# A third H buffer, stores queued ahead of zero fills, sums from tile 195, and a segment product from split F32R operands

## The chip, the core and the metric

The kernel runs on one core of a Trainium2 chip. A core has TensorE (PE), VectorE (DVE), ScalarE (ACT), GpSimd (POOL), SyncE (SP, which here only issues DMAs) and 16 DMA engines. The metric is the device time of one execution in microseconds (us).

## What is computed

Two graph layers over 50,000 nodes of 256 features and 25,000 edges sorted by target, each with a residual and a layer norm:

```python
neighbor_sum = segment_sum(x[col], row)            # edges -> their target nodes
mean_neighbor = neighbor_sum / max(deg, 1)
h_mean = (x + mean_neighbor) * 0.5 @ W_mean + b_mean
h_concat = concat([x @ W_ego + b_ego, mean_neighbor @ W_nb + b_nb])
gate = sigmoid(gate_weight * node_vec + gate_bias)
x = layernorm(x + (1 - gate) * h_mean + gate * h_concat)
# then an attention layer over the same edges (4 heads), and layernorm(x + it)
```

All of it is float32. What is changed here belongs to the first layer: the products of x (node tiles) and of the mean neighbour (edge tiles).

## The kernel before

**Stages.** A setup block loads weights and constants and starts sorting the edges. The node stage works on 391 node tiles of 128 rows. The edge stage behind it does the second layer and the outputs; the change leaves its code alone.

**Node tiles.** Tiles come in halves of HALF = 5, 78 halves and one last tile. SP loads a half of x into X (XB = 3 buffers, L468). TensorE transposes two tiles at a time (`turn`, L925), ACT copies them to xT (`copy_x`), TensorE multiplies each with w_node, 384 columns, into one of three PSUM banks (`product`, L937), which ACT has filled with the biases before (`seed`, L571). DVE adds x and the gated part into H (`first`, L665, and `add`, L677) and takes statistics (`stat`). H has two buffers of a half each; SP stores a finished half into hc_tab (`store`, L477). `first` waits, at the first tile of a half, until the store of the same buffer has landed.

**Zeros.** The other 384 columns of each row of hc_tab must be zero where a node has no edge. SP fills them from zero_row: rows 0 to 60 of each partition in the setup, then one `clear` (L482) for each half, 28 rows three times and then 7 rows each, by the table CLEARS. SP's order for half h is: load(h+3), clear(h+1), store(h). load(h+3) waits until half h has been read from X, store(h) until half h is complete. All three go on one hardware queue.

**Edge tiles.** 196 tiles of 128 edges, in 98 pairs. GpSimd gathers the edges' data (L518), then x[col] into xg (`fetch`, L522). DVE forms running sums acc (`run_sum`, L852). TensorE transposes a pair's sums into bank 4 (`turn_sum`, L963), ACT copies them to accT (`copy_sum`, L595), TensorE multiplies each tile with w_nb, 384 columns (`product_sum`, L973), ACT scales the result into cn (`main_part`, L602), and GpSimd scatters cn into hc_tab (`put`, L531). GpSimd's order is written out: put(t-13), then fetch(t). The first put waits until all zeros have landed.

**The order between the two.** The work on pairs is put by hand into the steps of the node tiles. A pair p begins at step SUMS + p * SPAN // 98, with SUMS = 188 and SPAN = 186: its running sums come in that step on DVE, its turn and copy two steps later (LATE = 2), its products two pairs after that (LAG_P = 2). From step FIX = 378 on a few instructions mend rows that cross partitions. DVE, ACT and TensorE each work through their steps in order, so an instruction that waits holds up all behind it on its engine.

Of the kernel before, what the change touches and what calls it, by code (L numbers as in the profile page):

```python
# [9 lines left out]
P, D = 128, 256  # L10
# [3 lines left out]
HALF = 5  # L14
# [79 lines left out]
def build(nc, x, src, dst, edge_weight, node_vec, W_mean, b_mean, W_ego, b_ego, W_nb, b_nb, gate_weight,  # L94
# [10 lines left out]
    with ExitStack() as ctx:  # L105
        def sb(n, s, d=F32):
            return ctx.enter_context(nc.sbuf_tensor(n, s, d))
# [35 lines left out]
        gwb = sb("gwb", [P, 2])  # L143
        w_node = sb("w_node", [P, 2, 384])
        w_nb = sb("w_nb", [P, 2, 384])
        w1f = sb("w1f", [P, 2, HEADS * HID])
        w1h = sb("w1h", [P, 2, HEADS * HID], F16)
        w1l = sb("w1l", [P, 2, HEADS * HID], F16)
# [38 lines left out]
        opened = sem("opened")  # L187

        c_zeroed = sem("c_zeroed")
        CLEARS = (0, 60, 88, 116) + tuple(range(144, NT, 7)) + (NT,)  # L190
        c_main = hc_tab[0:P * NT, 0:U].rearrange("(p t) d -> p t d", p=P)
        rows_merged, rec_out, ident_ready = sem("rows_merged"), sem("rec_out"), sem("ident_ready")
        XB = 3
        rows = ExitStack()
        X = [rows.enter_context(nc.sbuf_tensor(f"X{s}", [P, HALF, D], F32)) for s in range(XB)]
        x_in = [sem(f"x_in{s}") for s in range(XB)]
# [15 lines left out]
        with nc.Block() as block:  # L212
# [90 lines left out]
            def _(dve):  # L303
# [53 lines left out]
                st.wait()  # L357
                st.done(v.tensor_copy(w_nb[:, :, 0:256], w_node[:, :, 0:256]))
                st.wait()
                dve_at[0] = st.base + st.n  # L360

            @block.tensor
# [11 lines left out]


        TEN = 2 * HALF
        H = [tmp(f"H{s}", [P, HALF, HU]) for s in range(2)]
        XR = 4
        xT = [tmp(f"xT{b}", [P, 2, D]) for b in range(XR)]
        stats = tmp("stats", [P, TEN, 6])  # L380
        mv = tmp("mv", [P, TEN, 2])
        var_s = tmp("var_s", [P, TEN])
        sd_s = tmp("sd_s", [P, TEN])
        h_out = [sem(f"h_out{s}") for s in range(2)]
# [38 lines left out]
        accT = [tmp(f"accT{b}", [P, 2, D]) for b in range(AR)]  # L423
        carry = tmp("carry", [P, D])
        head_c = tmp("head_c", [P, U])
        carry_c = tmp("carry_c", [P, U])
# [8 lines left out]
        LASTR = (ET - 1) % AC  # L435
        PUT_LAG = 13

        SORT, PHASES, DECODE, SUMS, SPAN, FIX = 0, 7, 16, 188, 186, 378
        PRODS = (5, 6, 7)
        LEAD_X, LAG_P, LATE = 4, 2, 2  # L440

# [23 lines left out]
        with nc.Block() as block:  # L465
            @block.sync
            def _(sp):
                def load(h):  # L468
                    if h >= XB:
                        sp.wait_ge(a_done, (h - XB + 1) * HALF)  # L470
                    if h < 2 * ITER:
                        sp.dma_start(X[h % XB][:, :, :], x_main[:, h * HALF:(h + 1) * HALF, :])\
                            .then_inc(x_in[h % XB], 16)
                    else:
                        sp.dma_start(X[h % XB][:, 0, :], x[N - P:N]).then_inc(x_in[h % XB], 16)

                def store(j, s):  # L477
                    sp.wait_ge(h_done, j * TEN + (s + 1) * HALF)
                    sp.dma_start(h_main[:, bass.ds(j * TEN + s * HALF, HALF), :], H[s][:, :, :])\
                        .then_inc(h_out[s], 16)  # L480

                def clear(c):  # L482
                    lo, hi = CLEARS[c], CLEARS[c + 1]
                    sp.dma_start(c_main[:, lo:hi, :],
                                 zero_row[:, :].unsqueeze(1).to_broadcast([P, hi - lo, U])).then_inc(c_zeroed, 16)

                def half(j, s):
                    if 2 * j + s + XB <= 2 * ITER:
                        load(2 * j + s + XB)
                    if 2 * j + s < len(CLEARS) - 2:  # L490
                        clear(2 * j + s + 1)
                    store(j, s)

                for j in range(ITER):
                    for s in range(2):
                        half(j, s)
                for s in range(2):
                    sp.wait_ge(h_out[s], 16 * ITER)
                sp.wait_ge(h_done, NT + 1)
                sp.dma_start(hc_tab[N - P:N, U:RU], H[0][:, 0, :]).then_inc(h_out[0], 16)  # L500
                sp.wait_ge(h_out[0], 16 * ITER + 16)

            @block.gpsimd
            def _(pool):
# [55 lines left out]
            def _(act):  # L560
# [55 lines left out]
                def side(j, i):  # L616
                    now = j * TEN + i
                    if sorting(now):
                        m, part_ = phase_of(now)
                        if part_:  # L620
                            keep_upper(m)
                        else:
                            reverse_rows(m)
                            keep_back(m)
                    for p in tiles_of(now, LATE):
                        sums(p)
                    if now == FIX + 1:
                        act.wait_ge(carry_ready, 1)
                        a.activation(carry[:, :], bank[4][:, 0:D], ACT.Copy).then_inc(carry_out, 1)
                    if now == FIX + 3:  # L630
                        act.wait_ge(turned, PAIRS + 1)
                        a.activation(accT[0][:, 0, :], bank[5][:, 0:D], ACT.Copy).then_inc(turned_out, 1)

                def round_(j):
                    for i in range(TEN):
# [25 lines left out]
            def _(dve):  # L661
# [1 line left out]
                st = Steps(dve, dve1, dve_at[0])  # L663

                def first(t, i):  # L665
                    s, k = i // HALF, i % HALF
                    dve.wait_ge(p_ready, t + 1)
                    if t >= TEN and k == 0:
                        dve.wait_ge(h_out[s], (t - i) // TEN * 16)
                    if k == 0:  # L670
                        many = HALF if not isinstance(t, int) or t < NT else 1
                        v.tensor_copy(H[s][:, 0:many, D:D + 3], gates[:, bass.ds(t, many), :])
                    v.scalar_tensor_tensor(out=H[s][:, k, 0:D], in0=bank[NODE[t % 3]][:, 0:D],  # L673
                                           scalar=gates[:, bass.ds(t, 1), 1], in1=X[t // HALF % XB][:, k, :], op0=ALU.mult,
                                           op1=ALU.add).then_inc(a_done, 1)

                def add(t, i):  # L677
                    s, k = i // HALF, i % HALF
                    dve.wait_ge(a_done, t + 1)
                    v.scalar_tensor_tensor(out=H[s][:, k, 0:D], in0=bank[NODE[t % 3]][:, D:2 * D],  # L680
                                           scalar=gates[:, bass.ds(t, 1), 2], in1=H[s][:, k, 0:D], op0=ALU.mult,
                                           op1=ALU.add).then_inc(h_done, 1)

                def stat(t, i):
                    s, k = i // HALF, i % HALF
# [144 lines left out]
                def fix_degree():  # L830
# [31 lines left out]
                def side(j, i):  # L862
# [10 lines left out]
                        tables()  # L873
                    if now == DECODE + 2:
                        shares()
                    for p in tiles_of(now):
                        if p < PAIRS:
                            run_sum(2 * p, 2 * p % RS, 2 * p // RS)
                            run_sum(2 * p + 1, (2 * p + 1) % RS, 2 * p // RS)
# [3 lines left out]
                        {0: fix_rows, 2: fix_degree, 5: fix_sum}[now - FIX]()  # L883

                hround = [0]
                for s in range(2):
                    v.memset(H[s][:, :, D + 3:HU], 0.0)

                def round_(j):
                    hround[0] = j  # L890
# [31 lines left out]
            def _(pe):  # L922
# [40 lines left out]
                def turn_sum(p):  # L963
                    pe.wait_ge(acc_ready, 2 * p + 2)
                    if p:
                        pe.wait_ge(turned_out, p)
                    for t in (2 * p, 2 * p + 1):
                        for c in range(2):
                            o = t % 2 * D + c * P
                            ins = t_.transpose(bank[4][:, o:o + P], acc[t % AC][:, c * P:(c + 1) * P], ident[:, :])  # L970
                    ins.then_inc(turned, 1)

                def product_sum(t):  # L973
                    pe.wait_ge(turned_out, t // 2 + 1)
                    if t >= 3:
                        pe.wait_ge(cn_ready, t - 2)
                    for c in range(2):
# [24 lines left out]
                def product_carry():  # L1002
                    pe.wait_ge(turned_out, PAIRS + 1)
                    for c in range(2):
                        ins = t_.matmul(bank[6][:, 0:384], accT[0][:, 0, c * P:(c + 1) * P], w_nb[:, c, :],
                                        start=c == 0, stop=c == 1)
                    ins.then_inc(prod_ready, 1)

# [921 lines left out]
```

## Time and profile before

| | us |
|---|---|
| median of 3 runs | 2945.29 |
| the three runs | 2940.87, 2945.29, 7257.4 |
| profiled execution | 2944.66 |
| its span, first to last instruction | 2942.9 |
| mean granted TensorE clock in it | 0.973 of full |

The node stage takes about 27 to 1030 us of the span, the edge stage the rest. A time in the trace is counted from the start of the span. DMA share is the mean busy share of the 16 DMA engines as the packets' times add up, and can come out a little above 1.

### The profile page before, as it was taken

What the parts mean: (1) busy time and instruction counts of PE and PEld (TensorE: products, weight loads), DVE (VectorE), ACT (ScalarE), POOL (GpSimd) and SP (SyncE); (2) the same over time, 40 slices, a digit from 0 to 9 for tenths busy, and PEclk for the clock granted to TensorE, in tenths of its full rate; (3) what the DMA queues carried; (4) which work ended last, traced back from release to release, by engine and by line L of the source; (5) the groups of instructions that cost most, each with busy time, mean ns of one, the idle gap of its engine ahead of it and who ended that gap; (6) DMA issues with size and microseconds to landing.
All of it is one profiled execution on the core that took longest, in us unless ns stands there. A gap on an engine that the chain in (4) does not pass through costs nothing. (4 is left out here: it accounts for less than half of the span.)

```text
span 2942.9 us, 52181 instructions
## 1 busy us (share of the span) xinstructions
PE 2697.9 (92%) x13617; PEld 1554.7 (53%) x13617; DVE 2329.0 (79%) x7668; ACT 1851.3 (63%) x3839; POOL 1582.4 (54%) x1491
## 2 busy tenths in 40 slices
PE   4789889999999959999999999999999999976774
PEld 2455556666666525555555555555555555543442
DVE  8777775655565668888888888888888888878996
ACT  2344445555555437777777777777777777757885
POOL 0476717676666375455455454454554554405776
PEclk8799999999999979999999999999999999999998
DMA  9999995565555478777777787777777777647994
GB/s 339 304 301 314 306 308 182 187 192 180 182 189 189 143 182 218 215 223 214 213 227 214 213 221 216 215 218 217 219 217 212 226 213 212 193 118 241 278 278 154
DMA packets 544632, 653.46 MB, mean 222 GB/s; under 512 B 244302, under 2 KB 451850, under 8 KB 544518
## 3 DMA queue, kind: packets, MB, share of 16 engines
q1 hardware_dynamic: 468486, 440.38, 51.6%
q0 software_dynamic: 69472, 208.99, 22.7%
q10 hardware_dynamic: 6560, 2.84, 0.4%
q8 instruction: 40, 0.66, 0.1%
q14 instruction: 74, 0.61, 0.1%
HBM read 315.65 MB, written 299.10 MB: 209 GB/s over the span
## 5 line engine op out<-in xcount | busy, mean ns | idle before, releaser
L942 PE MATMUL bank<-w_node,xT 128*128 128x384 f32 x1564 | 568.5, 501 | 47.2 <-ACT bank L576 46.9
L1219 ACT ACTIVATE hidT<-bank,b1c 128x512 f32<-128x512 f32 x490 | 336.8, 687 | 414.5 <-PE bank L1509 340.7
L1128 POOL TENSOR_TENSOR u_hc<-u_hc 128x1536 f32<-128x1536 f32 x98 | 270.2, 2757 | 551.0 <-issue 429.0
L1509 PE MATMUL bank<-xh,w1h 128*128 128x512 f16 x1568 | 469.8, 381 | 23.1 <-DMA xh<-eh 15.7
L1509 PE MATMUL bank<-xl,w1h 128*128 128x512 f16 x1568 | 468.2, 380 | 0.0
L1509 PE MATMUL bank<-xh,w1l 128*128 128x512 f16 x1568 | 468.2, 380 | 0.0
L942 PEld LDWEIGHTS bank<-w_node,xT 128*128 128x128 f32 x1564 | 291.4, 195 | 227.7 <-ACT bank L576 61.6
L576 ACT ACTIVATE bank<-bias_all 128x512 f32<-128x512 f32 x391 | 234.3, 599 | 267.4 <-DVE H L680 266.2
L1525 PE MATMUL bank<-hidT,w2f 128*64 128x256 f32 x3136 | 360.1, 382 | 0.8 <-ACT hidT L1219 0.8
L1350 DVE STREAM_TRANSPOSE feat<-catT 32x256 f32<-32x256 f32 x784 | 342.5, 437 | 17.0 <-ACT catT L1228 2.4
L673 DVE SCALAR_TENSOR_TENSOR H<-bank,gates,X 128x256 f32<-128x256 f32 x391 | 187.2, 479 | 175.1 <-PE bank L942 172.5
L1331 DVE TENSOR_SCALAR hidT<-bank,b1c 128x512 f32<-128x512 f32 x294 | 220.7, 751 | 121.1 <-PE bank L1509 113.1
L535 POOL DMA_INDIRECT hc_tab<-cn,idx_s x196 | 201.1, 1026 | 192.8 <-ACT cn L606 76.6
L1525 PEld LDWEIGHTS bank<-hidT,w2f 128*64 128x64 f32 x3136 | 216.5, 137 | 141.4 <-issue 41.1
L978 PE MATMUL bank<-w_nb,accT 128*128 128x384 f32 x784 | 269.1, 486 | 0.0
L1509 PEld LDWEIGHTS bank<-xh,w1l 128*128 128x128 f16 x1568 | 154.0, 98 | 186.8 <-issue 3.1
L1509 PEld LDWEIGHTS bank<-xl,w1h 128*128 128x128 f16 x1568 | 153.8, 98 | 186.3 <-issue 1.7
L1115 POOL DMA_INDIRECT u_hc<-hc_tab,u_idx x196 | 191.6, 978 | 110.0 <-POOL u_idx L1111 80.1
L1682 POOL DMA_INDIRECT out_x<-zo,idx_s x196 | 204.4, 1043 | 85.3 <-issue 46.0
L1509 PEld LDWEIGHTS bank<-xh,w1h 128*128 128x128 f16 x1568 | 145.4, 98 | 181.2 <-issue 39.0
L527 POOL DMA_INDIRECT xg<-in_x,pay x196 | 191.3, 976 | 64.9 <-issue 56.1
L518 POOL DMA_INDIRECT pay<-rec_tab,ids_at x196 | 185.1, 944 | 72.0 <-issue 65.8
(248 smaller groups left out, 4833.0 us busy)
## 6 DMA issues: line engine op xcount, KB each, us to landing
hc_tab<-H SPq DMA_DIRECT2D x78, 680.0 KB, 7.9
er<-edge_tab SPq DMA_DIRECT2D x98, 512.0 KB
X<-in_x SPq DMA_DIRECT2D x78, 640.0 KB, 4.8
h_row<-hc_tab SPq DMA_DIRECT2D x97, 512.0 KB
out_x<-o_row SPq DMA_DIRECT2D x97, 512.0 KB, 5.0
hc_tab<-zero_row SPq DMA_DIRECT2D x35, 1344.0 KB, 8.4
edge_tab<-u_x SPq DMA_DIRECT2D x98, 256.0 KB
edge_tab<-feat SPq DMA_DIRECT2D x98, 256.0 KB
```

Source lines behind the costliest of these rows:

```text
L535: g.indirect_dma_start(out=hc_tab, out_offset=bass.IndirectOffsetOnAxis(idx_s[:, t, 2:3], 0), in_=cn[q][:, :], in_offset=None, bounds_chec ...
L576: a.activation(bank[NODE[t % 3]][:, :], bias_all[:, :], ACT.Copy).then_inc(seeded, 1)
L942: ins = t_.matmul(p[:, 0:384], xT[t // 2 % XR][:, t % 2, c * P:(c + 1) * P], w_node[:, c, :], start=False, stop=c == 1, skip_group_check=True)
L978: ins = t_.matmul(bank[PRODS[t % 3]][:, 0:U], accT[t // 2 % AR][:, t % 2, c * P:(c + 1) * P], w_nb[:, c, :], start=c == 0, stop=c == 1)
L1115: g.indirect_dma_start(out=u_hc[s][:, b, :], out_offset=None, in_=hc_tab, in_offset=bass.IndirectOffsetOnAxis(u_idx[:, s, b, 1:2], 0))\
L1128: g.tensor_tensor(c, c, u_hc[s][:, :, MULT:MULT + 3].unsqueeze(3).to_broadcast([P, 4, 3, P]), ALU.mult).then_inc(u_scaled, 1)
L1219: a.activation(hidT[m][:, :], bank[2 + m % 2][:, :], ACT.Relu, bias=b1c[:, m:m + 1])\
L1331: v.tensor_scalar(hidT[m][:, :], bank[2 + m % 2][:, :], b1c[:, m:m + 1], 0.0, ALU.add, ALU.max)\
L1350: ins = v.transpose(feat[s][e * 32:(e + 1) * 32, :, :] .rearrange("p b (h f) -> p h b f", h=HEADS)[:, :, :, at - FEAT:at - FEAT + 32], cat ...
L1509: ins = t_.matmul(bank[2 + m % 2][:, :], w[:, c, m * P:(m + 1) * P], xx[s][:, :, :].rearrange("p (k c) e -> p c k e", c=2)[:, c, :, :], st ...
L1525: ins = t_.matmul(bank[4 + k][side * FEAT:(side + 1) * FEAT, h * 2 * P:(h + 1) * 2 * P], w2f[:, m, :], hidT[m][:, side * 2 * P:(side + 1) ...
L1682: g.indirect_dma_start(out=out, out_offset=bass.IndirectOffsetOnAxis(idx_s[:, t, 3:4], 0), in_=zo[s][:, q, :], in_offset=None, bounds_chec ...
```

## The change

- H gets three buffers (HR = 3) in place of two, X four (XB = 4) in place of three.
- SP's order for a half becomes load(h+4), store(h), clear(h+1).
- The clears behind row 144 are of 6 or 7 rows in turn, 6.5 on the mean; the last one goes out with half 40 in place of half 38.
- SUMS goes from 188 to 195, SPAN from 186 to 177, FIX from 378 to 377.
- The segment product: w_nb is split once into w_nbh and w_nbl (F32R, high part and rest). ACT's copy of the transposed sums is written as F32R (accT); a new DVE instruction `low_sum`, in the step of the pair's turn, forms what is left of the sums (accL) from bank 4 and accT. `product_sum` then does six F32R matmuls of 384 columns in place of two f32 ones (each of which is two records in the trace): accT x w_nbh, accT x w_nbl, accL x w_nbh, for both halves of the 256 features. The next turn waits for `low_sum` in place of the copy.

```diff
-        CLEARS = (0, 60, 88, 116) + tuple(range(144, NT, 7)) + (NT,)
+        CLEARS = (0, 60, 88, 116) + tuple(144 + 13 * c // 2 for c in range(38)) + (NT,)
-        XB = 3
+        XB = 4
+                st.done(v.tensor_copy(w_nbh[:, :, :], w_nb[:, :, :]))
+                st.wait()
+                st.done(v.tensor_tensor(w_nbl[:, :, :], w_nb[:, :, :], w_nbh[:, :, :].bitcast(F32), ALU.subtract))
+                st.wait()
-        H = [tmp(f"H{s}", [P, HALF, HU]) for s in range(2)]
+        HR = 3
+        H = [tmp(f"H{r}", [P, HALF, HU]) for r in range(HR)]
-        SORT, PHASES, DECODE, SUMS, SPAN, FIX = 0, 7, 16, 188, 186, 378
+        SORT, PHASES, DECODE, SUMS, SPAN, FIX = 0, 7, 16, 195, 177, 377
-                def half(j, s):
-                    if 2 * j + s + XB <= 2 * ITER:
-                        load(2 * j + s + XB)
-                    if 2 * j + s < len(CLEARS) - 2:
-                        clear(2 * j + s + 1)
-                    store(j, s)
+                def half(h):
+                    if h + XB <= 2 * ITER:
+                        load(h + XB)
+                    store(h)
+                    if h < len(CLEARS) - 2:
+                        clear(h + 1)
-                    if t >= TEN and k == 0:
-                        dve.wait_ge(h_out[s], (t - i) // TEN * 16)
+                    if h >= HR and k == 0:
+                        dve.wait_ge(h_out[s], h // HR * 16)
+                def low_sum(p):
+                    dve.wait_ge(turned_out, p + 1)
+                    if p >= AR:
+                        dve.wait_ge(prod_ready, 2 * (p - AR) + 2)
+                    v.tensor_tensor(accL[p % AR][:, :, :], bank[4][:, :].rearrange("p (t d) -> p t d", t=2),
+                                    accT[p % AR][:, :, :].bitcast(F32), ALU.subtract).then_inc(low_out, 1)
+                    for p in tiles_of(now, LATE):
+                        if p < PAIRS:
+                            low_sum(p)
                     for p in tiles_of(now):
                         if p < PAIRS:
                             run_sum(2 * p, 2 * p % RS, 2 * p // RS)
...
                 def turn_sum(p):
                     pe.wait_ge(acc_ready, 2 * p + 2)
                     if p:
-                        pe.wait_ge(turned_out, p)
+                        pe.wait_ge(low_out, p)
...
                 def product_sum(t):
-                    pe.wait_ge(turned_out, t // 2 + 1)
+                    pe.wait_ge(low_out, t // 2 + 1)
...
                     for c in range(2):
-                        ins = t_.matmul(bank[PRODS[t % 3]][:, 0:U], accT[t // 2 % AR][:, t % 2, c * P:(c + 1) * P], w_nb[:, c, :],
-                                        start=c == 0, stop=c == 1)
+                        for part_, w in ((accT, w_nbh), (accT, w_nbl), (accL, w_nbh)):
+                            ins = t_.matmul(bank[PRODS[t % 3]][:, 0:U],
+                                            part_[t // 2 % AR][:, t % 2, c * P:(c + 1) * P], w[:, c, :],
+                                            start=n == 0, stop=n == 5)
+                            n += 1
```

## Rows read from the trace of the kernel before

**Rows 1.** Windows of three stages: each engine's busy us (instructions), clock, DMA
```profile
core 0: us, PE busy (x) PEld busy (x) DVE busy (x) ACT busy (x) POOL busy (x), PEclk, DMA share, GB/s
150.00:175.00 25.00, 22.59 (x91) 14.03 (x89) 17.03 (x60) 12.26 (x24) 18.90 (x21) 1.00 1.02 331
...
275.00:300.00 25.00, 23.53 (x93) 14.47 (x92) 18.32 (x64) 12.26 (x24) 18.91 (x21) 1.00 1.03 324
...
485.00:986.00 501.00, 501.00 (x1994) 319.23 (x1993) 298.26 (x951) 280.32 (x531) 338.95 (x339) 1.00 0.58 186
```

**Rows 2.** Waits from 100 to 430 us: us in total, times, longest
```profile
DVE H L672 <- DMA hc_tab<-H: 56.8, 26, 4.9
```

**Rows 3.** Timeline from 169 to 186 us: start, us, engine, line, idle before
```profile
170.25 0.46 SPq L484 DMA_DIRECT2D hc_tab<-zero_row  x1
...
170.75 0.64 SPq L479 DMA_DIRECT2D hc_tab<-H  x1
...
175.47 0.17 DVE L672 COPY H<-gates 128x15 f32<-128x15 f32 x1 [4.92 <-DMA hc_tab<-H]
```

**Rows 4.** Windows of 5 us: the stretch behind that wait
```profile
179.00:184.00 5.00, 5.00 (x14) 2.81 (x14) 3.51 (x11) 2.61 (x6) 3.78 (x5) 0.69 0.21 50
```

**Rows 5.** Timeline of SP's queue: stores of halves 3 and 38, last clear
```profile
120.86 0.56 SPq L479 DMA_DIRECT2D hc_tab<-H  x1
...
436.93 0.43 SPq L484 DMA_DIRECT2D hc_tab<-zero_row  x1
437.40 0.43 SPq L479 DMA_DIRECT2D hc_tab<-H  x1
```

**Rows 6.** DMA issues from 27 to 442 us: count, KB each, median us to landing
```profile
hc_tab<-zero_row SPq DMA_DIRECT2D x35, 1344.0 KB, 8.4
hc_tab<-H SPq DMA_DIRECT2D x39, 680.0 KB, 10.0
X<-in_x SPq DMA_DIRECT2D x39, 640.0 KB, 4.9
```

**Rows 7.** Timeline of PE from 700 to 706 us
```profile
701.89 1.46 PE L942 MATMUL bank<-w_node,xT 128*128 128x384 f32 x4
703.18 0.60 PE L970 MATMUL bank<-ident,acc 128*128 128x128 f32 x4
703.62 2.75 PE L978 MATMUL bank<-w_nb,accT 128*128 128x384 f32 x8
```

**Rows 8.** Groups of DVE: running sums, 485 to 985; 128x512 from PSUM, 1600 to 1900
```profile
L858 DVE SCALAR_TENSOR_TENSOR acc<-acc,same,xg 128x256 f32<-128x256 f32 x170 | 81.9, 481 | 12.0 <-DVE acc L858 1.0
...
L1331 DVE TENSOR_SCALAR hidT<-bank,b1c 128x512 f32<-128x512 f32 x57 | 42.8, 751 | 19.7 <-PE bank L1509 18.2
```

**Rows 9.** Timeline of POOL from 436 to 488 us: first put, first fetch, 17th put
```profile
442.43 1.04 POOL L535 DMA_INDIRECT hc_tab<-cn,idx_s  x1 [64.37 <-DMA hc_tab<-zero_row]
443.78 0.96 POOL L527 DMA_INDIRECT xg<-in_x,pay  x1 [0.30 <-issue]
...
484.32 1.02 POOL L535 DMA_INDIRECT hc_tab<-cn,idx_s  x1 [0.30 <-issue]
```

**Rows 10.** Timeline of DVE at the end of the setup
```profile
26.11 0.43 DVE L358 COPY w_nb<-w_node 128x512 f32<-128x512 f32 x1
```

**Rows 11.** Line of the gathers (L527): time from issue to landing
```profile
DMA to landing us min/median/max: 2.7/2.8/7.3
```

**Rows 12.** Timeline of PE near 1482 us, and weight loads from 485 to 985 us
```profile
1482.17 0.59 PE L1509 MATMUL bank<-xh,w1l 128*128 128x512 f16 x2
1482.60 0.59 PE L1509 MATMUL bank<-xl,w1h 128*128 128x512 f16 x2
...
L978 PEld LDWEIGHTS bank<-w_nb,accT 128*128 128x128 f32 x680 | 122.6, 190 | 67.5
```

**Rows 13.** Timeline of DVE: the last two running sums, the last H add
```profile
986.91 1.11 DVE L858 SCALAR_TENSOR_TENSOR acc<-acc,same,xg 128x256 f32<-128x256 f32 x2
...
1028.84 0.48 DVE L680 SCALAR_TENSOR_TENSOR H<-bank,gates,H 128x256 f32<-128x256 f32 x1
```

More of the change, by code:

```diff
@@ L145, in build @@
         w_nb = sb("w_nb", [P, 2, 384])
+        w_nbh, w_nbl = sb("w_nbh", [P, 2, 384], F32R), sb("w_nbl", [P, 2, 384], F32R)
         w1f = sb("w1f", [P, 2, HEADS * HID])
@@ L383, in build @@
         sd_s = tmp("sd_s", [P, TEN])
-        h_out = [sem(f"h_out{s}") for s in range(2)]
+        h_out = [sem(f"h_out{r}") for r in range(HR)]
         o_out = [sem(f"o_out{s}") for s in range(2)]
@@ L422, in build @@
         AR = 4
-        accT = [tmp(f"accT{b}", [P, 2, D]) for b in range(AR)]
+        accT = [tmp(f"accT{b}", [P, 2, D], F32R) for b in range(AR)]
+        accL = [tmp(f"accL{b}", [P, 2, D], F32R) for b in range(AR)]
+        carryT = tmp("carryT", [P, D])
+        low_out = sem("low_out")
         carry = tmp("carry", [P, D])
@@ L475, in load, with store @@
                         sp.dma_start(X[h % XB][:, 0, :], x[N - P:N]).then_inc(x_in[h % XB], 16)
[L477 to L480, printed above, removed]
+                def store(h):
+                    sp.wait_ge(h_done, (h + 1) * HALF)
+                    sp.dma_start(h_main[:, h * HALF:(h + 1) * HALF, :], H[h % HR][:, :, :]).then_inc(h_out[h % HR], 16)
                 def clear(c):
@@ L485, in clear @@
                                  zero_row[:, :].unsqueeze(1).to_broadcast([P, hi - lo, U])).then_inc(c_zeroed, 16)
-                def half(j, s):
-                    if 2 * j + s + XB <= 2 * ITER:
-                        load(2 * j + s + XB)
-                    if 2 * j + s < len(CLEARS) - 2:
-                        clear(2 * j + s + 1)
-                    store(j, s)
[L494 to L498, printed above, removed]
+                def half(h):
[4 more added lines that the diff above has]
+                        clear(h + 1)
+                for h in range(2 * ITER):
+                    half(h)
+                for r in range(HR):
+                    sp.wait_ge(h_out[r], 16 * len(range(r, 2 * ITER, HR)))
                 sp.wait_ge(h_done, NT + 1)
-                sp.dma_start(hc_tab[N - P:N, U:RU], H[0][:, 0, :]).then_inc(h_out[0], 16)
-                sp.wait_ge(h_out[0], 16 * ITER + 16)
+                r = 2 * ITER % HR
+                sp.dma_start(hc_tab[N - P:N, U:RU], H[r][:, 0, :]).then_inc(h_out[r], 16)
+                sp.wait_ge(h_out[r], 16 * len(range(r, 2 * ITER, HR)) + 16)
             @block.gpsimd
@@ L631, in side @@
                         act.wait_ge(turned, PAIRS + 1)
-                        a.activation(accT[0][:, 0, :], bank[5][:, 0:D], ACT.Copy).then_inc(turned_out, 1)
+                        a.activation(carryT[:, :], bank[5][:, 0:D], ACT.Copy).then_inc(turned_out, 1)
                 def round_(j):
@@ L665, in first @@
                 def first(t, i):
-                    s, k = i // HALF, i % HALF
+                    h, k = t // HALF, t % HALF
+                    s = h % HR
                     dve.wait_ge(p_ready, t + 1)
-                    if t >= TEN and k == 0:
-                        dve.wait_ge(h_out[s], (t - i) // TEN * 16)
+                    if h >= HR and k == 0:
+                        dve.wait_ge(h_out[s], h // HR * 16)
                     if k == 0:
@@ L677, in add @@
                 def add(t, i):
-                    s, k = i // HALF, i % HALF
+                    s, k = t // HALF % HR, t % HALF
                     dve.wait_ge(a_done, t + 1)
@@ L684, in stat @@
                 def stat(t, i):
-                    s, k = i // HALF, i % HALF
+                    s, k = t // HALF % HR, t % HALF
                     dve.wait_ge(h_done, t + 1)
@@ L885, in _ @@
                 hround = [0]
-                for s in range(2):
-                    v.memset(H[s][:, :, D + 3:HU], 0.0)
+                for r in range(HR):
+                    v.memset(H[r][:, :, D + 3:HU], 0.0)
                 def round_(j):
@@ L973, in product_sum @@
                 def product_sum(t):
-                    pe.wait_ge(turned_out, t // 2 + 1)
+                    pe.wait_ge(low_out, t // 2 + 1)
                     if t >= 3:
                         pe.wait_ge(cn_ready, t - 2)
+                    n = 0
                     for c in range(2):
-                        ins = t_.matmul(bank[PRODS[t % 3]][:, 0:U], accT[t // 2 % AR][:, t % 2, c * P:(c + 1) * P], w_nb[:, c, :],
-                                        start=c == 0, stop=c == 1)
+                        for part_, w in ((accT, w_nbh), (accT, w_nbl), (accL, w_nbh)):
[3 more added lines that the diff above has]
+                            n += 1
                     ins.then_inc(prod_ready, 1)
@@ L1004, in product_carry @@
                     for c in range(2):
-                        ins = t_.matmul(bank[6][:, 0:384], accT[0][:, 0, c * P:(c + 1) * P], w_nb[:, c, :],
+                        ins = t_.matmul(bank[6][:, 0:384], carryT[:, c * P:(c + 1) * P], w_nb[:, c, :],
                                         start=c == 0, stop=c == 1)
```

## The prediction

> **What bounds the kernel now.** I read the windows by stage first, then waits, transfers, and single rows of the stages the change touches. All of it lies in the node stage (from about 27 to 1030 us); the edge stage behind it is the same code.
>
> The node stage has two halves with different bounds. In its first half the 16 DMA engines are full (share 1.03 and 1.02, 324 and 331 GB/s) and TensorE is not [rows 1]. But that fullness is not steady. DVE waits 26 times, 56.8 us in all, for a store of H before it may write that buffer again [rows 2]. One case in detail: the clear is issued at 170.25, the store behind it at 170.75, and DVE idles 4.92 us until 175.47 for an H store that is behind another clear [rows 3]. While DVE waits, the queue runs empty, because SP only issues after a finished half: in 179 to 184 us the DMA share is 0.21 and the granted clock 0.69 [rows 4]. So the loop is: full queue, late store, idle DVE, empty queue. Stores are issued at 120.86 (half 3) and 437.40 (half 38), 9.04 us for each half [rows 5]. A half moves 640 + 680 + 1344 KB = 2.73 MB [rows 6], which at 324 to 331 GB/s takes 8.3 us.
>
> In the second half TensorE is busy 501.00 of 501 us, DMA share 0.58, DVE 298 us, ACT 280 us [rows 1]. A product of a node tile, four records of 384 columns, takes 703.18 - 701.89 = 1.29 us, so 0.323 each from start to start; four transposes take 703.62 - 703.18 = 0.44; the eight records of a pair's segment product take 8 x 0.323 = 2.58 [rows 7]. A node tile with its two transposes is 1.29 + 0.22 = 1.51. A pair of edge tiles comes each 186/98 = 1.898 steps: 0.44 + 2.58 + 1.898 x 1.51 = 5.89 us. Check: 501/5.89 = 85 pairs, and the trace has 170 running sums in that window [rows 8]. GpSimd is next: a put and a fetch follow each other without a gap from 442.43 to 484.32 in 16 rounds, 2.618 us each [rows 9], so 5.24 us a pair.
>
> **Three halves, stores ahead of zeros, smaller clears.** H gets a third buffer, so half h+3 and not h+2 waits for the store of h; that store now has one load ahead of it and no clear. From a finished half to the start of half h+3 are two halves, over 15 us; load and store (1.35 MB) need 4.2 us and up to one more half's work in the queue. I take the wait of [rows 2] as gone and ask what is late next: X is fetched four halves ahead, so not the loads; it is either the DMA rate or TensorE. Clears shrink from 7 to 6.5 rows a partition: a half is 640 + 680 + 1248 KB = 2.63 MB, 8.12 us at 324 GB/s and 7.95 at 331. TensorE needs 5 x 1.51 = 7.55. I take 8.12. Half 38 is then done at 120.9 + 35 x 8.12 = 405, plus 1.6 for the two DVE instructions added in setup (128x768 each; the 128x512 copy took 0.43 [rows 10], so 0.65 and about 0.9): 406.5. Bounds: 7.55 gives 387, and the old 9.04 scaled by bytes (8.71) gives 427.
>
> The last clear is issued after the store of half 40, tile 205. Steps 195 to 200 cost 1.62 each, steps 200 to 205 also carry sums at 2.83 (below): 406.5 + 8.1 + 14.2 = 429. Load, store and clear of that half are 2.5 MB, about 7 us. **Zeros landed: 436**, against 442.4 now, where the first put starts [rows 9] behind a clear issued at 436.93 [rows 5]. So the first half works 17 tiles further than now before the puts start, and still opens them 6 us sooner. This is the edit's gain; SUMS = 195 places the sums to match it. DVE will stand at step 205 for gather 13, which GpSimd issues right behind put 0: 436 + 1.35 + 2.8 landing [rows 9, 11] = 440. That is a stall of about 8 us, in the sum already; TensorE can run up to 3 tiles ahead in it and may lose clock for a few us as in [rows 4].
>
> **Segment product from split operands.** Four f32 records of 384 columns a tile go, six F32R ones come. The trace has no F32R matmul. Nearest row: f16 matmuls of 512 columns, each with its own weight load, start 0.43 us apart for two, 0.216 each [rows 12], 0.213 of that for 512 columns at 2.4 GHz. For 384 columns: 0.160 + 0.0025 = 0.1625 us. Above it lies the f32 record's 0.323 [rows 7], if F32R streams as slowly; between them 0.190, the time of one f32 weight load [rows 12], if loads do not hide. I take 0.1625: the f32 record's 0.323 is twice 0.160, so it looks like two passes over the columns, and one F32R record is one product of one part with one part, as one f16 record is. The Trainium skill's "FP8 and Floating Point Precision", TensorE Precision Notes, has true FP32 as four passes and reduced FP32 as one read cut to 22 bits. By it an F32R record would be a quarter of the 0.646 of an f32 product, 0.1615, an estimate, and the sum about 1 us shorter; no run here shows it yet.
>
> Pair on TensorE: 0.44 + 12 x 0.1625 = 2.39, and 177/98 = 1.806 steps at 1.51 = 2.73; together **5.12** (2.83 a step). That is now under GpSimd's **5.24**. The gain of 0.77 us a pair is cut to 0.65: GpSimd becomes the bound, narrowly.
>
> The subtraction (low_sum) is 128x512 from PSUM on DVE; the nearest is a TENSOR_SCALAR of that form, 751 ns [rows 8]. DVE has 298.26/85 = 3.51 us a pair [rows 1, 8], then 4.26 of 5.24. Queued behind it on DVE are the next pair's two running sums and the next tile's first(); it waits for ACT's copy, which waits for the turn. From a ready product: first, stat, add 1.1 us; the turn and ACT's copy are through at about 1.8; low_sum ends at 2.6, the running sums at 3.9, and the next product is ready at 2.39 + 1.29 = 3.7 to 4.1. So it fits, with little left. ACT's work is unchanged, 3.3 us a pair. TensorE waits for low_out only at the next turn.
>
> **Sum.** Last gather: 436 + 1.35 + 182 x 2.618 = 913.8, landed and summed from 916.7; now the last two running sums start at 986.91 and the last H add at 1028.84, 41.9 later [rows 13]. New tail: two tiles more (+3.0), three pairs' products shorter (3 x 0.63 = 1.9), a TensorE lead of about one tile (-2): 41.0, last add at 957.7. Gain 1028.8 - 957.7 = 71 us. The profiled execution took 2944.66 us (span 2942.9 and 1.8 around it), the median of the runs is 2945.29; 2944.7 - 71 = **2874**.
>
> **Rivals.**
> - The DMA queue doesn't stay full: another wait takes the place of the store's. SP standing in an issue, or the loads being late next, would do it; against it, 324 to 331 GB/s are held in whole windows [rows 1]. Half 8.71 us, zeros at 457: 2895. Chance 0.17.
> - Weight loads bound F32R: 12 x 0.190 = 2.28, pair 5.45, 91.4 pairs from 440: last sums at 934, 2892. Chance 0.10.
> - DVE becomes the bound through low_sum's place in its order: 5.5 us a pair, +25 us: 2899. Chance 0.13.
> - The subtraction holds GpSimd up, and GpSimd is the bound: 0.75 us a pair, 68 us, 2942. The puts keep 1.02 us and the gap of 0.30 beside DVE's work now [rows 9]. The Trainium skill's "SBUF — State Buffer", Who interferes with whom, has an exclusive port shared by VectorE and GpSimd, taken by two-port modes or by two SBUF inputs against a GpSimd read; this subtraction has one input in PSUM, so by that rule it costs nothing, and I keep a small chance only. 0.03.
> - Other side: F32R takes 0.323 as the f32 record does. Pair 0.44 + 3.88 + 2.73 = 7.05, last sums 164 us later and the tail 6: 3044. It decides from 0.239 us on, where a pair takes 6.04 and the gain is gone. For it speaks that both read 4 bytes an element, against it that the f32 record has twice the time of 384 columns at 2.4 GHz. Chance 0.05.
>
> **Chances.** The forecast itself has 0.52, with 2858 to 2888 as its own range. Faster by over 2% (about what a measurement of this kernel tells from no change) means under 2886: nearly all of the forecast and a quarter of the three middle rivals, 0.61. Slower by over 2%: 0.06. Within: 0.33. The range reaches from TensorE-bound first tiles (zeros at about 420) to past the DVE rival: 2852 to 2905.
>
> **What would show it.** DVE waits for hc_tab<-H near zero; stores 8.0 to 8.3 us apart to half 38; first put at 430 to 442; L978's successor 0.1625 start to start; puts and fetches without gaps to about 915 while TensorE falls below full; low_sum 0.75 us; last H add near 958. It is wrong if F32R records stand 0.19 or more apart, if puts wait for cn again, or if the first put comes after 450.

## The result and the profile after

The changed kernel takes 2864.38 us (median of 4 runs, 2864.33 to 2864.58) against 2943.51 for the kernel before beside it. The ratio is 0.9733, with a 95% interval of 0.9717 to 0.9748: 79 us are gained. One of the four executions behind 2943.51 took 7257.4 us and is left out of the ratio; without it their median is 2941.73 and the gain 77 us. The profiled execution took 2864.34 us, its span is 2862.5, and its last H add starts at 949.39 in place of 1028.84 [rows 13]. So 79.5 us come out of the node stage, and what lies behind its last H add is the same to within 1 us (1914.0 us before, 1913.2 now; in the profiled runs below it varies from 1912.5 to 1914.4, so that a difference of 1 us between two of them says nothing).

| | predicted | measured | kernel before |
|---|---|---|---|
| a half, us | 8.12 | 7.57 | 9.04 |
| half 38 done (store issued) | 406.5 | 387.45 | 437.40 |
| last clear issued | about 429 | 411.01 | 436.93 |
| first put | 436 | 420.42 | 442.43 |
| a put and a fetch, us | 2.618 | 2.622 | 2.618 |
| F32R record, start to start, us | 0.1625 | 0.175 | |
| last two running sums | 916.7 | 907.43 | 986.91 |
| last H add | 957.7 | 949.39 | 1028.84 |
| time | 2874 | 2864.4 | 2944.7 |

**First half.** First the windows of the changed kernel; columns as in [rows 1].

```profile
125.00:375.00 250.00, 250.00 (x994) 158.26 (x993) 222.23 (x794) 143.96 (x282) 178.37 (x190) 1.00 1.04 349
440.00:900.00 460.00, 459.81 (x2346) 369.68 (x2346) 349.70 (x1024) 280.96 (x531) 353.12 (x351) 1.00 0.64 204
407.00:410.00 3.00, 3.00 (x17) 2.02 (x15) 2.06 (x6) 1.54 (x4) 0.00 (x0) 1.00 0.04 14
419.00:422.00 3.00, 0.16 (x1) 0.00 (x0) 0.00 (x0) 0.00 (x0) 1.27 (x2) 1.00 0.00 0
425.00:435.00 10.00, 7.50 (x26) 6.55 (x27) 6.11 (x17) 3.40 (x7) 7.56 (x9) 0.60 0.33 102
```

From 125 to 375 us TensorE is busy all of the time, and DMA moves 349 GB/s. The same window of the kernel before has 28.65 us in which TensorE is idle, and 310 GB/s; the 324 and 331 of [rows 1] are its fuller stretches:

```profile
125.00:375.00 250.00, 221.35 (x842) 135.93 (x841) 185.60 (x672) 121.53 (x237) 180.17 (x192) 0.98 0.98 310
```

The queue of SP, half 3, half 38 and the last zeros:

```profile
122.64 0.37 SPq L488 DMA_DIRECT2D hc_tab<-H  x1
...
387.45 0.37 SPq L488 DMA_DIRECT2D hc_tab<-H  x1
...
411.01 0.53 SPq L492 DMA_DIRECT2D hc_tab<-zero_row  x1
```

35 halves lie between the two stores: 264.8 / 35 = 7.57 us each, against 9.04 [rows 5]. Five node tiles at TensorE's 1.51 are 7.55. The wait of [rows 2] has no row left between 100 and 430 us.

**Between the halves.** POOL's first put and first fetch, and then DVE's first running sums behind them:

```profile
420.42 1.04 POOL L543 DMA_INDIRECT hc_tab<-cn,idx_s  x1 [38.26 <-DMA hc_tab<-zero_row]
421.77 0.96 POOL L535 DMA_INDIRECT xg<-in_x,pay  x1 [0.30 <-issue]
```

```profile
424.54 1.10 DVE L874 SCALAR_TENSOR_TENSOR acc<-acc,same,xg 128x256 f32<-128x256 f32 x2 [9.06 <-DMA xg<-in_x,pay]
```

The puts start 22.0 us sooner than in [rows 9]. DVE stands for 9.06 us at step 205, for the gather that is issued behind the first put. This is the stall of the prediction (about 8 us). TensorE has work until 419.2 and is idle for 8.3 us, to 427.50. The granted clock falls while it is idle: it is 1.00 in the window from 419 to 422 us, 0.50 from 423 to 433 and so 0.60 on the mean from 425 to 435. In 407 to 410 us DMA moves next to nothing, 14 GB/s: the last zeros wait for half 40 to be finished, not for a full queue. At the lower of the two levels, 1.2 GHz, the first F32R records start 0.32 us apart (428.70, 429.02 and on to 431.90).

**Second half.** TensorE's timeline near 600 us, then its matmul and weight-load groups from 440 to 900 us (count, busy us, mean ns):

```profile
599.85 0.34 PE L999 MATMUL bank<-w_nbl,accT 128*128 128x384 f32 x1
600.02 0.34 PE L999 MATMUL bank<-w_nbh,accL 128*128 128x384 f32 x1
600.20 0.34 PE L999 MATMUL bank<-w_nbh,accT 128*128 128x384 f32 x1
600.38 0.34 PE L999 MATMUL bank<-w_nbl,accT 128*128 128x384 f32 x1
```

```profile
L999 PE MATMUL bank<-w_nbl,accT 128*128 128x384 f32 x348 | 117.2, 337 | 0.0
...
L999 PEld LDWEIGHTS bank<-w_nbl,accT 128*128 128x128 f32 x349 | 65.9, 189 | 0.0
```

An F32R record starts 0.17 to 0.18 us behind the one before it, 0.175 in the median of all (the sums below use 0.174, a difference of 0.01 us a pair), and its weights take 0.189 to load. That load is longer than the distance, so it is hidden beside the matmul before it. POOL's last put of this stretch and the last fetch, and DVE's last running sums and last H add:

```profile
897.61 1.02 POOL L543 DMA_INDIRECT hc_tab<-cn,idx_s  x1 [0.30 <-ACT cn L614]
898.93 0.97 POOL L535 DMA_INDIRECT xg<-in_x,pay  x1 [0.30 <-issue]
```

```profile
907.43 1.09 DVE L874 SCALAR_TENSOR_TENSOR acc<-acc,same,xg 128x256 f32<-128x256 f32 x2
...
949.39 0.48 DVE L689 SCALAR_TENSOR_TENSOR H<-bank,gates,H 128x256 f32<-128x256 f32 x1
```

182 puts after the first one, (897.61 - 420.42) / 182 = 2.622 us for a put and a fetch, so GpSimd goes at its own pace. But the last running sums come 8.5 us behind the last fetch, not the 2.9 of the prediction, and TensorE is busy 459.81 of 460 us. DVE's and GpSimd's waits in 440 to 900 us (us in total, times, longest):

```profile
DVE acc L874 <- DMA xg<-in_x,pay: 4.5, 7, 1.3
...
POOL hc_tab L543 <- ACT cn L614: 4.6, 15, 0.3
```

The second is no wait at all: it is 15 gaps of 0.30 us, the gap that GpSimd leaves between any two of its instructions. GpSimd goes at its own pace without a gap, and the first row says that DVE rarely waits for it, 4.5 us in all. So TensorE, busy throughout, is the bound here, with GpSimd less than 1% behind it.

### The profile page after: what moved, and what is told of

Same layout as the page of the kernel before. It is cut to its first block and busy times, and to the rows that moved or that the text cites. A ratio compares the mean times of both kernels' runs of the same rounds, so it can differ in the third digit from the quotient of the medians.

```text
span 2862.5 us, 53163 instructions
## 1 busy us (share of the span) xinstructions
PE 2641.2 (92%) x14009; PEld 1610.8 (56%) x14009; DVE 2393.4 (84%) x7769; ACT 1851.0 (65%) x3839; POOL 1582.5 (55%) x1491
## 5 line engine op out<-in xcount | busy, mean ns | idle before, releaser
L961 PE MATMUL bank<-w_node,xT 128*128 128x384 f32 x1564 | 558.6, 495 | 15.1 <-ACT bank L584 15.0
L1138 POOL DMA_INDIRECT u_hc<-hc_tab,u_idx x196 | 191.6, 978 | 110.0 <-POOL u_idx L1134 80.1
L1141 POOL DMA_INDIRECT u_hc<-hc_tab,u_idx x196 | 188.0, 959 | 64.9 <-issue 64.6
```

The lines of the kernel that those rows point to most:

```text
L961: ins = t_.matmul(p[:, 0:384], xT[t // 2 % XR][:, t % 2, c * P:(c + 1) * P], w_node[:, c, :], start=False, stop=c == 1, skip_group_check=True)
L1138: g.indirect_dma_start(out=u_hc[s][:, b, :], out_offset=None, in_=hc_tab, in_offset=bass.IndirectOffsetOnAxis(u_idx[:, s, b, 1:2], 0))\
```

## The experiments

"A" is the account of the prediction as the trace after had changed it: 3-deep H or the new order frees the stores, TensorE bounds the first half, the stall at step 205 is real time, and GpSimd (5.24 us a pair) and TensorE (5.26) bound the second half together. Each expectation splits it up into its own theory "A"; "B" is the rival of each run. In the text on each run, "last sums" are the last two running sums of DVE.

### The two parts apart

The product alone in the kernel before, with its two halves, its order, its clears and its SUMS:

```diff
+                    for p in tiles_of(now, LATE):
+                        if p < PAIRS:
+                            low_sum(p)
...
+                        for part_, w in ((accT, w_nbh), (accT, w_nbl), (accL, w_nbh)):
```

> The kernel before with the split F32R product and low_sum alone. Theory A (two independent gains): the first half is as before, first put at 442 us. The trace of the changed kernel has F32R records 0.174 us apart, so a pair takes TensorE 0.44 + 12 x 0.174 + 1.898 x 1.51 = 5.40 us against 5.89, above GpSimd's 5.24: 92 pairs save 45 us, time about 2898. Theory B (the product only pays together with the halves, because the subtraction makes DVE late): pairs stay above 5.6 us, time 2915 or more.

Measured: 2898.44 us, ratio 0.9853 (0.9837 to 0.987), so 43.2 us less than the 2941.6 beside it. The first put stays at 443.17; the last sums are at 943.0 in place of 986.91. From the sums behind the first gather (451.64) 91 pairs take 491.4 us, 5.40 each. The terms give 0.44 + 12 x 0.174 + 1.898 x 1.51 = 5.39. The old waits of the first half are all there, in the waits of that kernel from 100 to 430 us:

```profile
DVE H L680 <- DMA hc_tab<-H: 52.3, 26, 4.6
```

The node tiles and the order alone, with the old product:

```diff
-                            low_sum(p)
...
-                        for part_, w in ((accT, w_nbh), (accT, w_nbl), (accL, w_nbh)):
+                        ins = t_.matmul(bank[PRODS[t % 3]][:, 0:U], accT[t // 2 % AR][:, t % 2, c * P:(c + 1) * P], w_nb[:, c, :],
```

> The changed kernel with the old f32 segment product and without low_sum. Theory A: tile 195 is done near 388 us and the first put comes near 421, as in the changed kernel; pairs take TensorE 3.02 + 1.806 x 1.51 = 5.75 us, so the last sums start near 426 + 91.4 x 5.75 = 952 and the kernel takes about 2910. Theory B (tiles finished early are only a shift of the same work, because the second half is bound by TensorE anyway): 2930 or more.

Measured: 2905.07 us, ratio 0.9874 (0.9857 to 0.989), 36.5 us less, some 5 us under A's figure and far from B's. A half takes 7.59, the first put is at 418.30. 91 pairs from 422.39 to 946.08 take 5.75 us each; the terms give 0.44 + 2.58 + 2.73 = 5.75. The two parts together, 43.2 + 36.5 = 79.7, are the whole 79. That they add up fits their places one behind the other: one shortens the time before the puts, in which 206 node tiles are then done in place of 196, the other the pairs behind it. The new step table (SUMS, SPAN and FIX) was not run apart from the faster halves.

### Third H buffer or order

```diff
-        HR = 3
+        HR = 2
```

> The changed kernel with HR = 2 in place of 3: the store is ahead of its own half's zeros, but half h+2 waits for it. Theory A (the third buffer is what fills the queue): the store of h still stands behind the zeros issued with half h-1, so DVE waits again for hc_tab<-H, halves take 8 us or more, zeros land 10 to 25 us later, time 2872 to 2890. Theory B (the order alone does it): halves at 7.55 us, time 2864 to 2867.

```diff
                     if h + XB <= 2 * ITER:
                         load(h + XB)
-                    store(h)
                     if h < len(CLEARS) - 2:
                         clear(h + 1)
+                    store(h)
```

> The changed kernel with the zeros of a half ahead of its store, as before, and three H buffers. Theory A (the third buffer is what fills the queue): a store has over 15 us to land in place of 7.6, so halves stay at 7.55 us and the time at 2864 to 2868. Theory B (the order does it): DVE waits for stores, halves 8 us or more, 2872 or more.

Measured: two H buffers with the new order 2866.07 us (ratio 0.9743, 0.9727 to 0.976), three with the old order 2863.2 (0.973, 0.9714 to 0.9746). Neither differs from the change (2864.38) by more than 2 us. With two buffers A (the third buffer is what fills the queue) had asked for the wait's return and 2872 to 2890 us; it fell there, and B (the order alone does it) stands. With the old order A (three buffers are enough) stands. The waits of the kernel with two buffers, 100 to 430 us:

```profile
DVE H L681 <- DMA hc_tab<-H: 5.7, 6, 1.6
```

5.7 us remain of 56.8 [rows 2]. The halves take 7.61 us there ((388.52 - 122.28) / 35), 1.4 us more in all, which is about what the time shows. So both were undone together:

> The changed kernel with both undone: two H buffers and the zeros of a half ahead of its store; four X buffers, 6.5 rows of zeros and the rest stay. Each of the two alone undone left the time where it was (2866 and 2863). Theory A (either is enough to take the store out of DVE's way, both undone bring the wait back): DVE waits for hc_tab<-H some 50 us, halves 8.2 us or more, 2875 to 2890. Theory B (neither did it, the smaller clears or the fourth X did): 2863 to 2868.

Measured: 2906.53 us, ratio 0.9876 (0.9861 to 0.9891), 42 us more than the change. Its waits from 100 to 430 us, and its window from 125 to 375:

```profile
DVE H L681 <- DMA hc_tab<-H: 54.4, 25, 4.0
```

```profile
125.00:375.00 250.00, 221.64 (x847) 137.35 (x845) 186.03 (x671) 121.51 (x237) 181.90 (x193) 0.98 0.94 300
```

The wait is back in full, TensorE has 28 us of idle time in 250, and the rate falls to 300 GB/s with smaller clears. The first put is at 463.76, later than in the kernel before, because the last clear now goes out with half 40, whose last tile is done at 455.7 there. Either the third buffer or the order is enough, and only with both undone does the loop of [rows 3, 4] close again. A had the direction, but its price is larger than the 2875 to 2890 that A gave: the halves take 8.87 us.

The fourth X buffer:

```diff
-        XB = 4
+        XB = 3
```

> The changed kernel with three X buffers in place of four. Theory A (a full queue needs the fourth load's lead): TensorE waits for X, halves longer than 7.55 us, 2868 to 2885. Theory B (three halves' lead is enough, as no load was late before): 2862 to 2867.

Measured: 2864.97 us, 0.9732 (0.9717 to 0.9747). Nothing depends on it here, as B has it. It was run with the new clears only.

### The stall at step 205

Two ways take it away: puts that follow 16 fetches behind in place of 13, so that the gather of tile 13 needs no put ahead of it, and a last clear one half sooner.

```diff
-        PUT_LAG = 13
+        PUT_LAG = 16
```

> The changed kernel with PUT_LAG = 16: 16 gathers are issued before the first put, not 13. In the changed kernel DVE stood at step 205 from 415 to 425 us for gather 13, which GpSimd issues behind the first put. Theory A (that stall is real time, since TensorE is full behind it): step 205 goes on at once, the last sums start 8 to 11 us earlier, 2853 to 2857. Theory B (GpSimd, which starts at the same zeros, takes it back later): 2862 or more.

```diff
-        CLEARS = (0, 60, 88, 116) + tuple(144 + 13 * c // 2 for c in range(38)) + (NT,)
+        CLEARS = (0, 60, 88, 116) + tuple(144 + 246 * c // 37 for c in range(37)) + (NT,)
```

> The changed kernel with the zeros' last rows out with half 39 in place of 40: clears of 6 or 7 rows, 6.65 on the mean. Zeros then land near 408 in place of 420 us. Theory A: no stall at step 205, 2853 to 2857. Theory B (the DMA queue, at 350 GB/s in the changed kernel, has no room for 2.66 MB in 7.55 us): halves slow down and the gain is lost, 2860 or more.

Measured: 2857.11 us (0.971, 0.9697 to 0.9723) and 2854.56 (0.9699, 0.9686 to 0.9712). With a lag of 16 the first put is still at 420.68, but DVE no longer waits there:

```profile
415.78 1.10 DVE L874 SCALAR_TENSOR_TENSOR acc<-acc,same,xg 128x256 f32<-128x256 f32 x2
```

These sums stand at 415.78 in place of 424.54, 8.8 us sooner, and the last ones at 899.88 in place of 907.43, 7.6 sooner. A stands (2853 to 2857, just missed at its edge), but B has a small part in it: GpSimd starts as late as before, DVE still waits for gathers for 8.8 us behind it, 4.4 of them at 445.7, and TensorE is busy 446.75 of the 450 us from 440 to 890. With the clear one half sooner the first put is at 410.75 and the last sums at 898.96; DVE waits 1.41 us at step 205. If both took away different losses, both together would add up:

> Both mends of step 205 together: PUT_LAG = 16 and zeros out with half 39. Theory A (both remove the same stall): as the better of the two alone, 2852 to 2856. Theory B (the gathers also lack a lead later on, so that the two add up): 2850 or less.

Measured: 2853.98 us (0.9694, 0.968 to 0.9707), last sums at 896.4. A stands: it is the same stall, taken away twice. DVE waits for no gather any more, and TensorE is busy all of the time from 440 to 880 us.

### Did the smaller clears help

The old table, 7 rows a half and the last of them with half 38, in the changed kernel:

```diff
-        CLEARS = (0, 60, 88, 116) + tuple(144 + 13 * c // 2 for c in range(38)) + (NT,)
+        CLEARS = (0, 60, 88, 116) + tuple(range(144, NT, 7)) + (NT,)
```

> The changed kernel with the old table of zeros: 7 rows a half, the last row with half 38. Theory A (at 350 GB/s the queue is full, so 2.73 MB take 7.8 us): halves near 7.8 us, tile 195 some 6 us later, zeros at about 402 us and no stall at step 205: 2857 to 2862. Theory B (the queue has room): halves stay at 7.55 us, 2852 to 2856.

Measured: 2854.3 us (0.9694, 0.9679 to 0.9708), 10 us less than the change. Its window from 125 to 375 us, and GpSimd's first put:

```profile
125.00:375.00 250.00, 250.00 (x993) 158.03 (x992) 222.05 (x791) 143.80 (x281) 178.19 (x190) 1.00 1.05 360
```

```profile
403.36 1.04 POOL L543 DMA_INDIRECT hc_tab<-cn,idx_s  x1 [19.93 <-ACT cn L614]
```

B's account holds, the queue had room: the full 2.73 MB a half go through at 360 GB/s, TensorE is busy 250.00 of 250 us and a half takes 7.63, and the first put comes 17 us sooner, 1 us after the first products are scaled into cn (ACT ends at 402.38), so the zeros hold it by about 1 us at most. It is near the edge: in this kernel SP stands in the issue of a clear for 3.23 us near 382 us:

```profile
382.39 3.23 SPq L492 DMA_DIRECT2D hc_tab<-zero_row  x1
```

The smaller clears of the change give nothing and hold the puts back. Its last sums are at 896.50, as in the run before (896.4), though the first put is 8.5 us earlier: once the stall is gone, still earlier puts bring nothing, since 91 pairs from 415.98 take 5.28 us each by TensorE's steps.

### What an F32R matmul costs, and what bounds a pair

Four of the six matmuls over 256 columns in place of 384, which leaves 128 columns of their part of the product out:

```diff
+                            m = U if n in (0, 5) else 256
-                            ins = t_.matmul(bank[PRODS[t % 3]][:, 0:U], ... w[:, c, :],
+                            ins = t_.matmul(bank[PRODS[t % 3]][:, 0:m], ... w[:, c, 0:m],
```

> The changed kernel with four of the six F32R matmuls of a tile over 256 of 384 columns; the last 128 columns of these four products are left out. Theory A (the weight load of 128 columns sets the distance of F32R matmuls): starts stay 0.17 us apart and the time stays within 3 us of 2864. Theory B (the distance is the stream and a fixed cost): the four come at about 0.12 us, a pair takes TensorE 0.4 us less and GpSimd's 5.24 us becomes the bound, 2858 to 2861.

Measured, one run: 2857.08 us. TensorE's timeline in it:

```profile
601.61 0.28 PE L1000 MATMUL bank<-w_nbl,accT 128*128 128x256 f32 x1
601.73 0.28 PE L1000 MATMUL bank<-w_nbh,accL 128*128 128x256 f32 x1
601.85 0.28 PE L1000 MATMUL bank<-w_nbh,accT 128*128 128x256 f32 x1
...
602.09 0.34 PE L1000 MATMUL bank<-w_nbh,accL 128*128 128x384 f32 x1
602.26 0.34 PE L1000 MATMUL bank<-w_nbh,accT 128*128 128x384 f32 x1
```

A record of 256 columns is followed by the next one in 0.116 to 0.122 us, 0.118 in the median, well below the weight load, whose record is 0.192 in this kernel. A weight load of 0.19 therefore doesn't bound the matmuls, and A falls; the time is 1 us under B's 2858 to 2861. 256 columns at 2.4 GHz are 0.107, 384 are 0.160, so 0.011 us is left over at 256 columns and 0.015 at 384.

Four products a tile in place of six, without the one of accL (the low part of the sums is left out of the result):

```diff
-                        for part_, w in ((accT, w_nbh), (accT, w_nbl), (accL, w_nbh)):
+                        for part_, w in ((accT, w_nbh), (accT, w_nbl)):
```

> The changed kernel with four F32R matmuls a tile in place of six: the product of accL is left out, low_sum stays. A pair takes TensorE 0.44 + 8 x 0.174 + 2.73 = 4.56 us in place of 5.26. Theory A (GpSimd is a second bound, hardly below TensorE): put and fetch go on at 2.62 us a tile, TensorE idles, 2854 to 2859. Theory B (TensorE alone bounds the second half): 0.7 us a pair less, about 2800.

Measured, one run: 2860.53 us, only 3.9 less than the change, although 4 x 0.174 = 0.70 us of TensorE's work a pair is gone. B (about 2800) falls; A's 2854 to 2859 is missed by 1.5 us. The window from 440 to 900 us and the waits in it:

```profile
440.00:900.00 460.00, 420.02 (x2011) 322.63 (x2010) 347.41 (x1023) 274.03 (x534) 353.36 (x351) 0.96 0.63 201
```

```profile
DVE acc L874 <- DMA xg<-in_x,pay: 64.2, 34, 5.3
```

GpSimd takes 2.625 us a put and fetch in the run with 256 columns and 2.627 here, as in the change. TensorE is idle for 40 us, its granted clock falls to 0.96, and DVE waits 64.2 us for gathers. This run, with less work, gains less than the one with 256 columns (7.3 us). Of the 3.5 us between their spans 1.3 lie before the last sums (904.79 and 903.50), 1.0 between these and the last H add, and 1.2 behind it, in code that is the same; the clock may have made the first two, but with one run of each it stays open. As soon as TensorE has less to do, GpSimd, hardly faster, is the bound.

## Why the prediction held, step by step

**The wait and its mechanism: right, the cause too wide.** The waits for the store went, and what came next was named (the DMA rate or TensorE). The prediction credited the third buffer and the order together. The runs with one of them undone show that either is enough to within 2 us, and the one with both undone shows the wait again, 54.4 us.

**The half: the term that was mis-sized.** The prediction took the rate of the windows of before, 324 to 331 GB/s [rows 1], for the limit of the DMA engines: 2.63 MB gave 8.12 us. But these windows contain the very loop that the prediction had described, and their rate was that of the demand in it. The kernel before shows more in other places, in windows of 23 us (near the setup, with other transfers in the queue) and of 5 us (right ahead of [rows 4]):

```profile
27.00:50.00 23.00, 15.64 (x58) 9.55 (x58) 18.01 (x70) 9.88 (x21) 0.00 (x0) 0.82 1.06 374
```

```profile
174.00:179.00 5.00, 0.80 (x3) 0.61 (x3) 3.35 (x15) 0.90 (x2) 3.78 (x5) 0.97 1.07 375
```

The share of 1.02 and 1.03 looked like a limit; yet at 1.04 the changed kernel moves 349 GB/s and at 1.05 the one with seven rows moves 360. The lower bound of 7.55, TensorE's five tiles, was the answer. 35 halves x (8.12 - 7.57) = 19 us: half 38 was done at 387.45, not 406.5. The rival of a queue that doesn't stay full (8.71) had no part in it. The Trainium skill's "DMA: Bandwidth & Descriptors", Measured, has 425 GB/s in loads of 16 MB issued from GpSimd on a core whose neighbour is idle, and about 358 for each where both cores of a memory's domain stream. The first no run here shows. By either of them 324 was no ceiling; the 360 measured here over 250 us, and the 375 over 5, do not tell where it lies.

**From half 38 to the puts: nearly right.** Steps 195 to 205 took 23.2 us (387.45 to 410.60), against 8.1 + 14.2 predicted. The zeros took 9.4 us behind the issue of the last clear, against about 7. The 7 was too small by the prediction's own figures: the last clear has 7 rows, so load, store and clear are 640 + 680 + 1344 KB, 2.73 MB and not 2.5, 8.4 us at 324 GB/s. So the first put came 15.6 us before its 436. The "17 tiles further" were miscounted too: 196 node tiles are done at the first put in the kernel before and 206 in the changed one, 10 more.

**The stall at step 205: right and under-used.** 9.06 us against about 8. The prediction carried it in its sum as if it had to be. It also counted the smaller clears as a saving of bytes and did not compare them with the old table: at TensorE's pace the bytes cost nothing, and the two halves more until the last clear cost the stall. The runs price that at 10 us.

**F32R: right in kind, 0.0125 us too small.** One pass at 2.4 GHz is right: 0.175 for 384 columns, 0.118 for 256. What lies between records is 0.011 to 0.015, not the 0.0025 of the f16 records. The rival at 0.190 falls by the run with 256 columns (its price had a slip: 440 + 91.4 x 5.45 is 938, not 934, so its time should have been about 2895), the other side's 0.323 by the timeline. The Trainium skill's "FP8 and Floating Point Precision", TensorE Precision Notes, with four passes for true FP32, fits: 0.646 / 0.175 = 3.7.

**Who bounds the pair: wrong, narrowly.** GpSimd's 5.24 is right, but TensorE's pair is 0.44 + 12 x 0.174 + 2.73 = 5.26, not 5.12, and TensorE is the bound. The prediction's sign that TensorE falls below full failed: 459.81 of 460. From the stall's end 91 pairs took 907.43 - 424.54 = 482.9 us, 5.31 each. In the two runs in which TensorE never stands, both mends together and the old table of clears, they take 5.28. In the change the 2.4 us on top are about what the low clock costs, by an estimate from its records: 12 of them 0.32 apart in place of 0.175, and the tiles beside them. With one mend alone they take 5.32 (lag of 16) and 5.29 (clear sooner); there the clock is full, and TensorE idles for 3.3 and 1.6 us between 440 and 880 us. The last sums lag 8.5 us behind the last fetch, not 2.9, because they come at TensorE's pace and no longer wait for the gather, which has landed after some 3 us. The stall has no part in that: the lag is 8.5 in the runs with one mend too.

**DVE and the subtraction: right.** `low_sum` took 0.690 us in the median (0.75 predicted), TensorE waited for it 0.2 us in 440 to 900, and DVE had 349.70 us of work in 460, 4.00 a pair (4.26 predicted). The median distance of a put from the next is 2.595 us with the subtraction, and 2.596 in the run without it: it costs GpSimd nothing. This is what the rule of the Trainium skill's "SBUF — State Buffer", Who interferes with whom, on the port shared by VectorE and GpSimd gives for one input in PSUM.

**The sum.** Against the prediction: last fetch 14.9 us earlier (the halves, less the longer landing of the zeros), lag of the sums 5.6 longer, tail 42.0 in place of 41.0. -14.9 + 5.6 + 1.0 = -8.3, as the last H add shows (949.39 against 957.7). The gain of 79 against 71 is so two misses of opposite sign, the larger one in a rate that was taken from a disturbed window. That the time came within 10 us and not 15 is luck: the second miss, the wrong engine as the bound, made up for part of the first.

**A better version.** Four full versions beat both kernels. Behind the lag of 16 alone (2857.11) three are better still: the old table of clears in the changed kernel (2854.3), a last clear one half sooner (2854.56), and that with a put lag of 16 (2853.98). They don't differ from each other by what these runs can tell. The first needs least: it is the change without its new clears. That XB = 4 can go as well was shown with the new clears and not with the old table. Beyond it TensorE (5.28 us a pair) and GpSimd (5.24) would have to be shortened together.

## What to carry to other kernels

A transfer rate that is read in a window with a feedback wait in it is the demand of that loop, not the limit: size the new stage by the next engine's pace as well, and let the rate be an upper bound of the time only. Where two engines stand within 1% of each other, work out what the second one allows: taking 0.70 us a pair off one of them brought 4 us of 91 x 0.70 = 64, as the other one allows no more than 91 x (5.28 - 5.24). And where work is made smaller to fit a queue, ask what waits for the last piece of it; here smaller pieces and more of them cost 10 us.

## What the runs showed of the hardware

- The packets' share of the DMA engines is no measure of room at the top: 1.02 stood beside 331 GB/s, 1.04 beside 349, 1.05 beside 360 and 1.07 beside 375.
- F32R matmuls that load 128x128 weights each follow one another at the columns' time at 2.4 GHz plus 0.011 us (256 columns) to 0.015 us (384), beside weight loads of 0.189 to 0.193 us each, longer than the distance itself.
- A DMA issue can hold SP. In the kernel before the first three stores, each issued behind a clear of 28 rows, take 12.8, 11.3 and 11.9 us to issue; with three H buffers and the zeros first they take up to 11.9, and the time is no longer than with the store first, where no store takes over 1.2.
- TensorE stood for 8.3 us at step 205. The granted clock fell to the 1.2 GHz level while it stood, and was 0.60 on the mean of the 10 us from 425 to 435.
